# Two state buffers, two early orders rewritten and a one-to-one end in a fused graph-layer and mixture-of-experts kernel

## The reference

```
x: 16 graphs x 512 nodes x 128, adj: 16 x 512 x 512 (0/1)
xl = layernorm(x)
conv = relu(bn(conv17(relu(bn(conv1(xl))))) + xl)        # along the nodes
s = xl @ w_se + b_se;  A = exp(-|s_i - s_j|^2) * adj
nmp = A @ relu(xl @ w_msg + b_msg)
r, z, n = GRU gates of [conv, nmp] and xl
x = x + (1 - z) * n + z * xl                             # the state
xn = layernorm(x) * gamma + beta
top 2 of 8 experts by xn @ Wr + br, weights by softmax
x = x + sum over the 2 of w * (gelu(xn @ W1[e] + b1[e]) @ W2[e] + b2[e])
```

## Time and profile before

| what | value |
|---|---|
| median of the runs | 614.63 us |
| profiled execution, its time | 613.4 us |
| profiled execution, its span | 611.6 us |
| PE busy | 587.0 us (96%) |
| DVE, ACT, POOL busy | 478.4, 366.6, 339.5 us |
| mean granted PE clock | 0.992 |

### The profile page before, as it was taken

How to read it: one execution, slowest core, us unless ns; L and a number is a source line. 1 busy time by engine, 2 the same in 40 slices (tenths; PEclk the granted TensorE clock), 3 DMA queues, 4 the chain that set the end, 5 groups by cost and what they waited for, 6 DMA issues and landing times. The chain is left out here.

```text
span 611.6 us, 12890 instructions
## 1 busy us (share of the span) xinstructions
PE 587.0 (96%) x3936; PEld 515.5 (84%) x3936; DVE 478.4 (78%) x2014; ACT 366.6 (60%) x733; POOL 339.5 (56%) x249
## 2 busy tenths in 40 slices
PE   8999999999999999999999999999999999999991
PEld 6887778786879797979898989898898979999890
DVE  7978888898788988898989797979787966644330
ACT  5644637365858484848485767666675745655540
POOL 2000505133367577777776767778686563555765
PEclk9999999999999999999999999999999999999996
DMA  8519171725466757566666656657556778666853
GB/s 298 200 65 331 48 258 57 241 66 177 122 191 145 194 128 207 127 177 156 173 163 155 159 162 157 182 140 187 146 153 148 214 163 239 139 154 134 224 96 43
DMA packets 85861, 99.72 MB, mean 163 GB/s; under 512 B 7521, under 2 KB 62561, under 8 KB 85473
## 3 DMA queue, kind: packets, MB, share of 16 engines
q1 hardware_dynamic: 64064, 82.37, 43.3%
q0 software_dynamic: 21728, 16.53, 16.8%
HBM read 74.95 MB, written 30.39 MB: 172 GB/s over the span
## 5 line engine op out<-in xcount | busy, mean ns | idle before, releaser
L1013 POOL DMA_INDIRECT out<-y_t,xt x88 | 160.4, 1823 | 85.4 <-DMA out<-y_t,xt 53.0
L1048 POOL DMA_INDIRECT routed<-row,at_u x112 | 116.9, 1043 | 140.4 <-DVE at_u L1255 109.0
L570 PE MATMUL C<-cv_h,w_hi 128*128 128x256 f32 (+1 forms) x432 | 129.1, 299 | 3.3 <-ACT tz L926 1.5
L571 PE MATMUL C<-cv_l,w_hi 128*128 128x256 f32 (+1 forms) x432 | 123.4, 286 | 0.0
L572 PE MATMUL C<-cv_h,w_lo 128*128 128x256 f32 (+1 forms) x432 | 123.3, 286 | 0.0
L570 PEld LDWEIGHTS C<-cv_h,w_hi 128*128 128x128 f32 x432 | 81.7, 189 | 7.2 <-issue 3.2
L571 PEld LDWEIGHTS C<-cv_l,w_hi 128*128 128x128 f32 x432 | 81.5, 189 | 0.9
L572 PEld LDWEIGHTS C<-cv_h,w_lo 128*128 128x128 f32 x432 | 81.5, 189 | 0.7
L749 PE MATMUL G<-ex,msg_t 128*128 128x512 f32 x128 | 58.2, 597 | 1.7 <-ACT gh L945 1.7
L651 PE MATMUL Y<-w_t,ge 128*128 128x128 f32 x424 | 55.8, 274 | 0.0
L651 PEld LDWEIGHTS Y<-w_t,ge 128*128 128x128 f32 x424 | 51.7, 191 | 3.1 <-issue 2.6
(11 more groups left out here) (273 smaller groups left out, 1614.3 us busy)
## 6 DMA issues: line engine op xcount, KB each, us to landing
w_t<-w_all SPq DMA_DIRECT2D x63, 392.0 KB, 3.6
adj<-adj_t SPq DMA_DIRECT2D x16, 1024.0 KB, 5.8
xt<-routed SPq DMA_DIRECT2D x63, 144.0 KB, 2.4
wd<-w_all SPq DMA_DIRECT2D x11, 392.0 KB, 5.2
x_ln<-x SPq DMA_DIRECT2D x16, 256.0 KB, 2.8
x_res<-x_t SPq DMA_DIRECT2D x16, 256.0 KB, 6.0
out<-x SPq DMA_DIRECT2D x15, 256.0 KB, 3.9
w_all<-w_s SPq DMA_DIRECT2D x1, 3136.0 KB, 9.7
```

The lines of the kernel that those rows point to most:

```text
L570: pe.matmul(psum, hi(w), rhs_h, start=start, stop=False)
L571: pe.matmul(psum, hi(w), rhs_l, start=False, stop=False)
L1013: nc.gpsimd.indirect_dma_start(out=out, out_offset=bass.IndirectOffsetOnAxis(ap=xt[j][:, t, R_ID:R_ID + 1].bitcast(U32), axis=0), in_=y_t[ ...
L1048: nc.gpsimd.indirect_dma_start(out=routed, out_offset=bass.IndirectOffsetOnAxis(ap=ats_u[d % 2][:, n:n + 1], axis=0), in_=rows[d % 2][:, n ...
```

## The change

- The state buffer `x1` becomes two, `x1s[d % 2]`, each with its own store semaphore `out_set[i]`; ACT waits for the store and the router of graph d - 2 instead of d - 1.
- PE runs all nine blocks of `conv_sum` before `states` (before: five, `states`, four).
- PE computes HH+2 (`product_hn`, for ACT's `gh`) first of the three gate products in graphs 0 to 14.
- DVE adds into `tr` before it computes `gr` from `x_res`.
- The sixteen bias products of graph 1 are spread in pairs over eight places of graphs 1 and 2; their sum on DVE, and the store of the expert weights `w_all` (3136 KB) that needs it, move from graph 1 to graph 3. The two large stores of padding rows move one graph earlier.
- In the end the items alternate tile, dense, tile, dense, from the first on, and 13 dense items are left behind the last tile. SP may load eight tiles ahead, and waits only for what frees the buffer (`pe_y` and `own_done` of the tile eight before; for the first eight, `added`, since their buffers hold tiles whose adds read them). The waits for `added` six tiles back and for `add_begun` go.
- The padding rows behind each expert's region (8 small stores) are issued as soon as the counts are there, ahead of the first dense weights and the wait for the table; only one dense load goes ahead of the tile loads instead of three.

```diff
--- before.py
+++ after.py
@@ -44,16 +44,13 @@
 TILES = ROUTED * NODES * TOP // TILE + EXPERTS - 1
 STREAMED = SLOTS * (GRAPHS - FIRST)
 LAST = TILES - STREAMED
-SPACED = 4
-LANDED = 6
-AHEAD = 5
+AHEAD = RING
 EARLY = 3
-FRONT = 4
 DENSE_LOADS = ([(e, (0,)) for e in range(EARLY)] + [(e, (0, 1)) for e in range(EARLY, EXPERTS)] +
                [(e, (1,)) for e in range(EARLY)])
 TAKEN = SLOTS * TILE
...
@@ -252,9 +249,9 @@
         nn = sb("nn", [P, NODES])
         x1T = sb("x1T", [P, NODES])
         xc = nn
-        x1 = sb("x1", [P, NT, STATE])
-        x1_d = [sb(f"x1_d{i}", [P, NT, STATE]) for i in range(DENSE - 1)] + [x1]
+        x1s = [sb(f"x1_{i}", [P, NT, STATE]) for i in range(2)]
+        x1_d = [sb(f"x1_d{i}", [P, NT, STATE]) for i in range(DENSE - 1)] + [x1s[1]]
         w_d = [sb(f"w_d{i}", [P, NT, EXPERTS]) for i in range(DENSE)]
         rows = [sb(f"row{i}", [P, NT, ROW]) for i in range(2)]
         xnT = sb("xnT", [P, NODES])
...
@@ -424,9 +416,11 @@
         def loads_in_order():
-            at = [(last_of_load(k - DENSE_BUFFERS), 1, k) for k in range(DENSE_BUFFERS, len(DENSE_LOADS))]
-            at += [(number.get(n - AHEAD, STREAMED), 0, n) for n in range(STREAMED, STREAMED + LAST)]
-            return [entry[1:] for entry in sorted(at)]
+            at = [(last_of_load(k - DENSE_BUFFERS), TILES, 1, k) for k in range(DENSE_BUFFERS, len(DENSE_LOADS))]
+            at += [(STREAMED, STREAMED + k - 1, 1, k) for k in range(1, DENSE_BUFFERS)]
+            at += [(number.get(n - AHEAD, STREAMED), n, 0, n) for n in range(STREAMED, STREAMED + LAST)]
+            return [entry[2:] for entry in sorted(at)]
         def run(iteration):
             for g in range(GRAPHS):
...
@@ -456,7 +450,7 @@
             sp.dma_start(w_s[:, :, X_W2:X_W2 + 2 * P].bitcast(F32),
                          weights[:, W2 * P:(W2 + 16) * P].rearrange("p (e h) -> p e h", e=EXPERTS)).then_inc(w2_loaded, 16)
             sp.dma_start(routed[DUMMY:DUMMY + TAKEN, :], pads[0:TAKEN, :]).then_inc(pads_stored, 16)
-            sp.dma_start(out[TOKENS:TOKENS + TAKEN, :], pads[0:TAKEN, 0:P]).then_inc(out_set, 16)
+            sp.dma_start(out[TOKENS:TOKENS + TAKEN, :], pads[0:TAKEN, 0:P]).then_inc(pads_stored, 16)
             def tile_loads(j, at, e):
                 sp.dma_start(xt[j][:], routed[bass.ds(at, TILE), :].rearrange("(t p) c -> p t c", p=P)).then_inc(
...
@@ -485,7 +479,7 @@
                         sp.wait_ge(added, 16 * TT * (n - RING + 1))
                     tile_loads(slot, *chosen[j])
-                if g == 1:
+                if g == 3:
                     sp.wait_ge(w12_ready, 2)
                     sp.wait_ge(w2_loaded, 16)
                     sp.wait_ge(b1_set, 1)
...
@@ -499,7 +493,7 @@
                     if moe:
                         batch_load(g, 3)
                     if d < ROUTED:
-                        sp.dma_start(out_v[d], x1[:, :, 0:P]).then_inc(out_set, 16)
+                        sp.dma_start(out_v[d], x1_of(d)[:, :, 0:P]).then_inc(out_set[d % 2], 16)
                 if g < GRAPHS - 2:
                     sp.wait_ge(xl_ready, g + 2)
                     sp.dma_start(x_ln[:], x_v[g + 2]).then_inc(x_ln_loaded, 16)
...
@@ -512,39 +506,37 @@
                 sp.dma_start(x_res[:], x_t[g]).then_inc(x_res_loaded, 16)
                 if g == FIRST - 1:
                     sp.wait_ge(w12_stored, 16)
-                    sp.wait_ge(pads_stored, 48)
+                    sp.wait_ge(pads_stored, 64)
                 if FIRST - 1 <= g < GRAPHS - 1:
                     chosen[:] = [choice(g % 2, j) for j in range(SLOTS)]
                     for i in range(2):
                         sp.wait_ge(rows_out[i], 16 * NT * TOP * ((g - i) // 2))
                     for j in range(2):
                         batch_load(g + 1, j)
+                if g == 1:
+                    sp.dma_start(routed[DUMMY + TAKEN:, :], pads[TAKEN:, :]).then_inc(pads_stored, 16)
                 if g == 2:
-                    sp.dma_start(routed[DUMMY + TAKEN:, :], pads[TAKEN:, :]).then_inc(pads_stored, 16)
-                if g == 3:
                     sp.dma_start(out[TOKENS + TAKEN:, :], pads[TAKEN:, 0:P]).then_inc(pads_stored, 16)
             chosen = []
             run(iteration)
-            for k in range(DENSE_BUFFERS):
-                dense_loads(k)
-            sp.wait_ge(tab_step, TAB_STEPS * (ROUTED - 1 - TAB_FIRST) + LAST_STEPS)
+            sp.wait_ge(tab_step, TAB_STEPS * (ROUTED - 1 - TAB_FIRST) + 2)
             for e in range(EXPERTS):
                 at = sp.value_load(t_pad[0:1, e:e + 1], min_val=e * REGION, max_val=e * REGION + TOKENS)
                 sp.dma_start(routed[bass.ds(at, TILE), :], pads[0:TILE, :]).then_inc(pads_stored, 16)
+            dense_loads(0)
+            sp.wait_ge(tab_step, TAB_STEPS * (ROUTED - 1 - TAB_FIRST) + LAST_STEPS)
             for i in range(2):
                 sp.wait_ge(rows_out[i], 16 * NT * TOP * ((ROUTED + 1 - i) // 2))
-            sp.wait_ge(pads_stored, 16 * (EXPERTS + 3))
+            sp.wait_ge(pads_stored, 16 * (EXPERTS + 4))
             def last_loads(n):
                 at, e = choice(2, n - STREAMED)
-                if n < STREAMED + LANDED:
-                    sp.wait_ge(added, 16 * TT * (n - LANDED + 1))
+                if n < STREAMED + RING:
+                    sp.wait_ge(added, 16 * TT * (n - RING + 1))
                 else:
-                    sp.wait_ge(add_begun, n - LANDED - STREAMED + 1)
-                if n >= STREAMED + RING:
                     sp.wait_ge(pe_y, number[n - RING] + 1)
                     sp.wait_ge(own_done, n - RING + 1)
                 tile_loads(n % RING, at, e)
...
@@ -685,24 +678,30 @@
                 if is_graph(g, 1):
                     pe.wait_ge(wr_set, 2)
                     pe.wait_ge(w1_loaded, 16)
-                    for n in range(16):
-                        last = pe.matmul(H0[:, n:n + 1], w1_raw[:, n * P:(n + 1) * P], vec[:, V_BETA:V_BETA + 1],
-                                         start=True, stop=True)
-                    last.then_inc(pe_b1, 1)
+                def bias_products(first):
+                    if is_graph(g, 1) or is_graph(g, 2):
+                        for n in range(first + 2 * (g - 1), first + 2 * g):
+                            last = pe.matmul(H0[:, n:n + 1], w1_raw[:, n * P:(n + 1) * P], vec[:, V_BETA:V_BETA + 1],
+                                             start=True, stop=True)
+                        last.then_inc(pe_b1, 1)
                 tile_a(0)
+                bias_products(0)
                 if is_graph(g, 0):
                     pe.wait_ge(w_lo_done["conv_s"], 1)
                     pe.wait_ge(w_lo_done["conv_a"], 1)
                 pe.wait_ge(odd_split, g + 1)
                 if tail:
                     pe.wait_ge(gate_step, 2 * d + 2)
-                conv_sum(0, 5)
+                conv_sum(0, TAPS_A)
                 if tail:
                     pe.wait_ge(x1T_ready, d + 1)
                     pe.wait_ge(s_f32, g + 1)
                     states(STATES)
-                conv_sum(5, TAPS_A)
                 tile_b(0)
+                bias_products(4)
                 pe.wait_ge(msg_f32, g + 1)
                 pe.wait_ge(xlT_f32, g + 1)
                 transposes(M, msg_f).then_inc(pe_msgT, 1)
...
@@ -726,6 +723,7 @@
                 tile_a(1)
                 conv_diff(4, 14)
                 tile_b(1)
+                bias_products(8)
                 conv_diff(14, TAPS)
                 if tail and d >= ROUTED:
                     pe.wait_ge(xn_ready, d + 1)
...
@@ -734,11 +732,17 @@
                 if is_graph(g, 0):
                     pe.wait_ge(w_lo_done["gates"], 1)
                 pe.wait_ge(exp_done, NT * g + NT)
+                def product_hn():
+                    product(G0[:], HH + 2, xlT_h[:], xlT_l[:]).then_inc(pe_hn, 1)
+                if d < ROUTED:
+                    product_hn()
                 product(G1[:], HH + 1, xlT_h[:], xlT_l[:], stop=False)
                 product(G2[:], HH, xlT_h[:], xlT_l[:], stop=False)
-                if tail and d >= ROUTED:
+                if d >= ROUTED:
                     pe.wait_ge(xnT_f32, d - ROUTED + 1)
-                product(G0[:], HH + 2, xlT_h[:], xlT_l[:]).then_inc(pe_hn, 1)
+                    product_hn()
+                bias_products(12)
                 if more:
                     pe.wait_ge(xl_ready, g + 2)
                     transposes(M, flat(xl)).then_inc(pe_xT, 1)
...
@@ -859,10 +863,9 @@
             def states(d, banks):
                 act.wait_ge(pe_outT, d + 1)
-                if x1_of(d) is x1:
-                    act.wait_ge(out_set, 16 * min(d, ROUTED) + 16)
-                    if d > 0:
-                        act.wait_ge(rt_step, router_first(min(d, ROUTED) - 1) + 1)
+                if d >= 2 and x1_of(d) is x1s[d % 2]:
+                    act.wait_ge(out_set[d % 2], 16 * (d // 2))
```

(22 more changed lines are left out.)

40 lines of the change are left out of this document (18 added, 22 removed).

## The result

The changed kernel takes 618.18 us (median of 8 runs, 617.36 to 620.22) against 615.58 (8 runs, 614.16 to 616.4) for the kernel before on the same chip: ratio 1.0055, 95% interval 1.0042 to 1.0068. It is slower by 2.6 us; I had forecast 608.8, range 604.0 to 613.5. The two profiled executions stand further apart, at 613.4 and 619.21: that of the kernel before is faster than every one of its eight runs, and that of the changed kernel lies 1.0 above its median.

What follows compares the result with a forecast made beforehand. PE's early waits, its full middle and GpSimd's adds at the end were taken to bound the kernel. Early 3.5 gained, middle 0.5 lost, end 2.8 gained: 5.8 us off, median 614.63 to 608.8, range 604 to 613.5.

Steps and rivals of the forecast that it cites:

- The gain per early graph: Early graphs: `tr` first gives 0.60 us and HH+2 first 0.16, so 0.76 each in graphs 3 and 4.
- The middle: Eleven graphs with tiles: later state products use up tz's 0.54 us margin; 0.05 us lost each, 0.5 in all.
- PE's end near 599: Last stage: PE waits longer at the passage and ends near 599, a microsecond later than before.
- The late four waits: Last stage: GpSimd's four later landing waits find the queue quiet and fall towards 2.45 us, 1.9 us gained.
- Traffic of the end: Last stage: 19 tiles and some six dense loads between 496 and about 543 us, some 270 GB/s.
- The second buffer, its semaphores and the moved stores cost and give nothing: Early graphs: ACT's state copies never waited for a store, and the `w_all` store has time to land; size zero.
- The chain of 38: Last stage: GpSimd's 38 adds start at 512.2 instead of 516.69, 4.5 us earlier.
- The passage's idle: Entry to the last stage: PE waits some 2.8 us for DVE's split instead of 1.14.
- the first four: Last stage: GpSimd's first four of eight landing waits take 3.4 us each, bounds 2.45 and 3.90; 3.6 us lost.
- My own sign of being wrong: Last stage: the prediction is wrong if GpSimd's first landing waits exceed 4.1 us.
- the end gives nothing: Rival, last stage: first four waits of 4.1 to 4.8 us eat the gains; 611.6 to 614.6 us, chance 0.17.
- The rival: Last stage: loads running ahead of GpSimd hold back its adds, four waits of 6 us; 619.4 us, chance 0.05.

Runs made afterwards that it cites:

- early_core: Kernel before plus two state buffers and the early order of PE and DVE, `tr` ahead of `gr` included; 613.34 us, ratio 0.9961.
- states_split: Kernel before plus two state buffers, moved stores, spread bias products and `tr` ahead of `gr`, with PE's old order; 612.75 us, ratio 0.9956.
- stores_end: Changed kernel with the early order of PE and DVE put back to that of the kernel before; 621.58 us, ratio 1.0109.
- front_two: Changed kernel with two dense items ahead of the first last tile in PE's order; 628.9 us, ratio 1.0215.
- after_third: Changed kernel unchanged, run again as the base of the fourth submission; 630.62 us, ratio 1.0185.
- end_gated_2: Changed kernel with the tile loads' wait for GpSimd's adds (`add_begun`) put back, new order kept, second run; 626.6 us, ratio 1.011.
- early_only_2: Changed kernel with the whole last stage put back to that of the kernel before, second run; 624.43 us, ratio 1.0081.
- end_only: Kernel before plus two state buffers and the new last stage alone; 621.62 us, ratio 1.0091.
- before_again: Kernel before unchanged, run again in the second submission; 616.98 us.
- three_bufs: Changed kernel with three state buffers instead of two; 628.16 us, ratio 1.0184.
- store_late: Changed kernel with the `w_all` store issued in graph 3 behind the loads of x_ln and x_res; 629.59 us, ratio 1.021.
- early_core_2: Second run of early_core, in the fifth submission: kernel before plus two state buffers and the early order; 625.73 us, ratio 1.0148.

## Why the prediction was wrong

**Right.** The gain per early graph: forecast 0.76 us (0.60 + 0.16), measured 0.72 (26.83 to 26.11 in early_core), and no `gh` wait of PE. The two steps can be told apart: from graph 3 to 4 the kernel before takes 26.79, states_split with `tr` first 26.27, and early_core with HH+2 first as well 26.11, so 0.52 and 0.16. The middle: PE busy 340.00 of 340, period from graph 5 to 14 31.93 against 31.91; I had allowed 0.05 a graph. PE's end near 599. The late four waits: 1.7 us gained, forecast 1.9. Traffic of the end from 496 to 543 us: 260 GB/s at a share of 0.93, forecast 270; tile 62's load came at 547, where I had 543 less the early gain.

**Sizes off.** Up to `nn` of graph 1 I had 1.88 us; the traces show 2.77 (1.11 up to graph 0, and 29.23 - 27.57 = 1.66). Graph 2, with two pairs of bias products in it, lost 0.44 (27.27 against 26.83), where I had 0.1.

**Failed, early.** "The second buffer, its semaphores and the moved stores cost and give nothing ... the w_all store has graphs 3 and 4 to land." I asked who waits for the store, and nobody does. I did not ask what is queued behind it: 256 KB of x_ln behind 3136 KB, wanted by DVE 3.8 us after its issue (111.36 - 3.14 - 104.38). In the changed kernel graph 3 takes 30.10 us, and graph 4, without a store, 26.21: 3.9 us. Of these 2.5 stand in states_split too (28.75 - 26.27), which has no clock drop, and in stores_end (29.37 - 26.84 = 2.5); the other 1.4 come beside the clock at 0.51. In these two traces the early part therefore gave nothing: `nn` of graph 4 starts at 150.0 against 149.7, where I had 3.5 us.

**Failed, end, first add.** "The chain of 38 starts at 512.2 instead of 516.69": it starts at 516.44. I moved the tile's result earlier and left GpSimd's add of tile 43 at 506.14, as if the new loads did not fly beside the adds ahead of the list. Two of those waits are now 4.32 and 4.06, where they were 2.62 and 2.87, tile 43 is added at 510.16, and the 4.5 us are gone but for 0.3. The new loads are not the whole of it, for the 2.87 was at the short end: over nine traces with the old end the same wait goes from 2.8 to 4.7 us. The rows of the kernel before and of early_core:

```profile
499.64 1.57 POOL L1013 DMA_INDIRECT out<-y_t,xt  x1 [2.62 <-DVE y_t L1358]
```

```profile
507.22 1.55 POOL L1018 DMA_INDIRECT out<-y_t,xt  x1 [4.68 <-DMA out<-y_t,xt]
```

With the old end a long wait there delays nothing, since the first add of the list comes 16.3 to 16.7 us behind `nn` of graph 15 in every such trace; the forecast gain hung on it. The passage's idle, forecast at 2.8, measured 2.42; front_two, with 0.79, is no faster by its ratio (1.0215 against the changed kernel's 1.0195 and 1.0185).

**Failed, end, waits.** "For the first four the bounds are 2.45 and 3.90 from these rows; I take 3.4." They average 4.38 (17.5 us against 10.0 before). The row of 3.90 came from a place with a DMA share of 0.78 and 232 GB/s; the end ran at 1.00 and 295 while the first of these waits passed. I took the nearest loaded row for an upper bound, though I had myself worked out more traffic than it had. My own sign of being wrong, "if the first waits exceed 4.1 us", has come true. The size, 4.38, is the one that my rival "the end gives nothing" has (4.1 to 4.8 us, chance 0.17); its time was too low, since it kept the 4.5 us of the first add.

**The rival** that happened is the one that ends on the other side, loads that run ahead hold back the adds' landing, to which I gave 0.05. I counted four waits and let it decide at 4.8 us each; six waits bear it, and 4.4 were enough, since the gains that stood against it were not there. That it is the loads is shown twice in one submission: against after_third's 18.3 us the first four waits fall to 12.0 with the gate alone put back (end_gated_2), and to 9.9 with the whole stage (early_only_2). The Trainium skill (DMA: Bandwidth & Descriptors, section Queues, rings and completion order) says that a DMA's semaphore write waits for earlier writes of the same DMA engine, whichever queue they are in. The traces agree with it: for adds of unchanged size GpSimd waits 2.4 us at a share of 0.31 and 5.9 to 6.7 at 1.00. They can't tell it from engines that are merely shared. I had quoted the rule and priced it at nothing, on one wait of 2.87 us.

**Sums.** In the two profiled executions: early and middle 3.0 forecast, -0.2 measured by graph 15; end 2.8 forecast, -5.7 measured. That is 5.8 us slower. By the medians it is 2.6, and the new end alone costs 6.0 (end_only) or 6.2 (after_third against early_only_2). If the parts add up, the early part and the middle gave 3.4 us in the median run, where I had 3.0, and the end is the whole miss: 2.8 forecast, -6.0 measured. That the early sum comes out is partly luck, for I had neither the 2.5 us that the store costs in graph 3 nor a loss of the kernel before that the change removes: in before_again the clock falls to 0.50 behind the bias products of graph 1 and the graph takes 30.66 us, 1.4 more than in the trace that I had:

```profile
44.60:48.00 3.40, 3.40 (x18) 3.40 (x17) 3.34 (x6) 0.68 (x3) 0.00 (x0) 0.50 0.51 204
```

No trace with the products spread over two graphs has this drop. How many runs of the kernel before have it is not known; at 1.4 us it covers less than half of the 3.2 us between traces and medians, and the rest is open.

## What to carry to other kernels

Before moving a large store, look at what its queue issues next and by when that must land; that nobody waits for the store itself says nothing. A wait between loads and read-modify-write stores may look like needless coupling and be what keeps the stores' landing short: on a chain of dependent adds, price the landing at the traffic that the change makes, not at the traffic of the trace. And when an earlier start is claimed, follow the serial engine from one step ahead of the claimed place, with every wait repriced. Before two traces are compared, see where each stands among the runs of its kernel: here they were 5.8 us apart and the medians 2.6.

## What the runs showed of the hardware

- Late finishes. On four of six occasions TensorE's products in graphs 2 and 3 raised their semaphores up to 4.8 us after their recorded ends, in every kernel with the early changes, and 0.8 to 1.0 us late in the kernel before. The recorded matmuls run at their usual pace up to that point, and from graph 4 on it is under 1.4 us or gone. The traces of those occasions also hold fewer semaphore updates (7,133 to 7,586, against 10,170 to 10,217 in the others), so the occasions differ in more than the kernel. The chip alone doesn't decide it: the second submission, with late finishes, and the third, without, both ran on chip number 5. The cause is open; it is worth 9 to 12 us here.
- The clock. Behind each PE idle of 3.88 us or more in graphs 2 and 3 the granted clock went to the 1.2 GHz level. Behind shorter ones it did so in some traces and not in others of the same work: at the passage, behind idles of 2.42 to 2.57 us, it fell in seven traces and stayed in three (2.57 in stores_end, 2.48 in three_bufs, 2.43 in store_late); in graph 3 it fell behind 1.23 and 1.39 us in the changed kernel and stayed behind 0.58 and 1.41 in states_split. So one trace with a drop or without is no price of an idle.
- The clock and one-column products. In early_core it fell near 43.9 with no idle ahead of it, a little behind the one-column bias products, which count as busy:

```profile
39.03 3.63 PE L691 MATMUL H<-vec,w_raw 128*128 128x1 f32 x32
```

```profile
36.00:43.60 7.60, 7.60 (x55) 7.01 (x54) 6.81 (x10) 6.02 (x10) 0.00 (x0) 1.00 0.01 2
43.60:47.10 3.50, 3.50 (x20) 3.50 (x20) 3.07 (x6) 0.00 (x0) 0.00 (x0) 0.55 0.61 242
```

Of the five traces with all sixteen products in graph 1 three have this drop (early_core, early_core_2, before_again) and two haven't (the kernel before, end_only); of the fifteen with the products spread in pairs none has.
- Loads at a DMA share of 1.00 stretch GpSimd's wait for the landing of unrelated 128-row adds from 2.4 to as much as 6.7 us.
